# Expert rows of a routed layer: gathered in quarters of the tokens and transposed by VectorE instead of TensorE

## The reference, cut to what matters

```python
scores = jnp.maximum(x @ gate_W + gate_b, 1e-4)
p = softmax(scores)                       # 8 experts, the best 2 are kept
w = maximum(p, 0.1) / (sum of the two kept)
y = einsum('bsd,edf->bsef', x, expert_W) + expert_b
out = einsum('bsef,bse->bsf', y, comb) / 2
x = x + out
```

## Time and profile before

| | before |
|---|---|
| median of three runs | 1190.6 us |
| the profiled execution | 1190.14 us, span 1188.3 us |
| mean granted TensorE clock | 0.984 |
| PE / DVE / ACT / POOL busy | 1148.8 / 587.7 / 308.7 / 462.5 us |
| part from the first expert matmul to the end | from 896.5 us of the span |

### The profile page before, as it was taken

How to read it: one execution, slowest core, us unless ns; L and a number is a source line. 1 busy time by engine, 2 the same in 40 slices (tenths; PEclk the granted TensorE clock), 3 DMA queues, 4 the chain that set the end, 5 groups by cost and what they waited for, 6 DMA issues and landing times.

```text
span 1188.3 us, 15152 instructions
## 1 busy us (share of the span) xinstructions
PE 1148.8 (97%) x5588; PEld 984.9 (83%) x5588; DVE 587.7 (49%) x1171; ACT 308.7 (26%) x416; POOL 462.5 (39%) x394
## 2 busy tenths in 40 slices
PE   6999999999999999999999999999959999999996
PEld 5898888888788999999988878888847788788884
DVE  7935666555332122211133447997589622744444
ACT  2421212133111121211022213343353411623232
POOL 0003457457787577511000015233323444443433
PEclk9999999999999999999999999999968999999998
DMA  9382785783634444477457633463288954876653
GB/s 355 114 347 50 204 226 117 232 210 36 137 48 43 93 93 94 97 159 153 92 175 244 204 109 116 166 243 131 94 297 307 336 87 91 257 235 128 190 88 72
DMA packets 115835, 192.15 MB, mean 162 GB/s; under 512 B 33960, under 2 KB 63912, under 8 KB 114624
## 3 DMA queue, kind: packets, MB, share of 16 engines
q1 hardware_dynamic: 81008, 159.53, 39.0%
q0 software_dynamic: 34768, 31.82, 19.8%
HBM read 136.19 MB, written 61.68 MB: 167 GB/s over the span
## 4 chain that ended last, share of the span: by engine, by line
PE 89%; DVE 8%; issue 1%; ACT 1%; DMA 0%; DVEq 0%; POOL 0%; ACTq 0%; POOLq 0%
PE ps L1564 28%; PE ps L1565 28%; PE ps L1566 28%; DVE e_lo L1389 2%; PE ps L1783 2%; PE ps L1712 2%; PE ps L1652 2%; DVE xn_lo L1116 1%; DVE stats L1088 1%; DVE acc L1104 1%; PE ps L1610 1%; DVE y L1534 0%; ACT lt_hi L1012 0%; DMA acc<-in_x 0%; DVE tok_w L1503 0%
## 5 line engine op out<-in xcount | busy, mean ns | idle before, releaser
L734 POOL DMA_INDIRECT cnt_d<-times,addr_i x160 | 263.0, 1644 | 179.1 <-DMA cnt_d<-times,addr_i 96.0
L1564 PE MATMUL ps<-e_hi,lt_hi 128*128 128x512 f32 x368 | 148.0, 402 | 2.8 <-DVE e_lo L1389 2.3
L1566 PE MATMUL ps<-e_hi,lt_lo 128*128 128x512 f32 x368 | 144.1, 392 | 0.0
L1565 PE MATMUL ps<-e_lo,lt_hi 128*128 128x512 f32 x368 | 144.1, 391 | 0.0
L1565 PE MATMUL ps<-xt_lo,q_hi 128*128 128x416 f32 (+1 forms) x384 | 135.0, 352 | 0.0
L1564 PE MATMUL ps<-xt_hi,q_hi 128*128 128x416 f32 (+1 forms) x384 | 135.0, 351 | 0.0
L1566 PE MATMUL ps<-xt_hi,q_lo 128*128 128x416 f32 (+1 forms) x384 | 134.6, 351 | 0.0
L842 POOL DMA_INDIRECT out<-y,row_put x46 | 73.7, 1602 | 87.8 <-ACT y L1046 51.4
L1564 PEld LDWEIGHTS ps<-e_hi,lt_hi 128*128 128x128 f32 x368 | 69.6, 189 | 23.2 <-DVE e_lo L1389 9.0
L1257 DVE TENSOR_TENSOR qs<-ps,qs 128x416 f32<-128x416 f32 (+1 forms) x24 | 14.2, 592 | 136.9 <-PE ps L1566 136.9
L1566 PEld LDWEIGHTS ps<-e_hi,lt_lo 128*128 128x128 f32 x368 | 69.5, 189 | 14.9
(11 more groups left out here) (257 smaller groups left out, 2382.0 us busy)
## 6 DMA issues: line engine op xcount, KB each, us to landing
e_raw<-in_L_ffn_expert_W SPq DMA_DIRECT2D x64, 512.0 KB, 9.8
cnt_d<-zeros SPq DMA_DIRECT2D x20, 640.0 KB, 12.2
rows<-key_d SPq DMA_DIRECT2D x8, 1250.0 KB, 7.5
acc<-in_x SPq DMA_DIRECT2D x18, 512.0 KB, 7.5
w_raw<-in_L_mix_w_key SPq DMA_DIRECT2D x16, 512.0 KB, 4.4
cnt_d<-cnt_d POOLq DMA_DIRECT2D x10, 640.0 KB, 7.6
cnt<-cnt_d SPq DMA_DIRECT2D x10, 640.0 KB, 5.9
h_d<-hs SPq DMA_DIRECT2D x18, 256.0 KB, 2.3
```

Source lines behind the costliest of these rows:

```text
L734: nc.gpsimd.indirect_dma_start(out=cnt_d[i], out_offset=bass.IndirectOffsetOnAxis(ap=addr_i[:, j:j + 1], axis=0), in_=times[:, j:j + 1], i ...
L1564: nc.tensor.matmul(o, lh, rh, start=(k == 0), stop=False)
L1565: nc.tensor.matmul(o, lh, rl, start=False, stop=False)
L1566: return nc.tensor.matmul(o, ll, rh, start=False, stop=(k == last_k))
```

## The change

The rows stored in HBM have their 1024 columns in another order, so that each row falls into four pieces of 256 columns: piece q holds columns 32q to 32q+31 of every group of 128. The gate's weights are loaded in a matching order, by eight DMAs instead of one. In the loop, POOL gathers a block in four indirect DMAs of 128 pieces of 1 KB. The t-th of them is for tokens 32t to 32t+31, and brings to partitions 32q to 32q+31 the q-th pieces of these tokens. The 32x32 transposes of VectorE, 256 columns at a time and straight into PSUM banks 4 and 5, then give the whole transposed block. The indices for this (`quad_of`) come from four small matmuls with shifted unit matrices (`sel`). TensorE's transposes leave the loop. Only the first block is still gathered whole; ACT puts its columns back in order (`gp`) in two copies, and TensorE transposes it.

The small copies of indices (`tok_now`, `row_put`) go from POOL to DVE. In DVE's loop, the four transposes, each with its copy of the next indices, stand at the start of an iteration, ahead of the bias of the left half. POOL's loop holds six indirect DMAs and waits only. In SP's stream one weight piece of the third expert waits for the first block's transposes, because `gp` is stored in its place.

The diff, cut to its core:

```diff
+    QD = 32
+    NQD = P // QD
+    QK = D // NQD
+        sel = at("sel", X + HALF, [P, NQD, P], f16)
+        gp = at("gp", RING + (2 * KB - 1) * D, [P, KB, P])
 # SP
                     if running is not None and k == AT_ONCE:
-                        sp.wait_ge(s_gx, first_block[running] * 16 + 32)
+                        sp.wait_ge(s_gx[NQD - 1], first_block[running] * 16 + 16)
...
-                    sp.dma_start(gw[:, :, :], gate_W.rearrange("(k p) e -> p k e", p=P)).then_inc(s_gw, 16)
+                    for c in range(NQD):
+                        for g in range(2):
+                            sp.dma_start(gw[c * QD:(c + 1) * QD, g:KB:2, :],
+                                         gate_W[(g * NQD + c) * P:(g * NQD + c + 1) * P, :].rearrange("(q i) e -> i q e", q=NQD)).then_inc(s_gw, 16)
...
-            sp.wait_ge(s_gx, 16)
-            load_expert(2, range(KB))
+            sp.wait_ge(s_gx[0], 16)
+            load_expert(2, range(KB - 1))
+            sp.wait_ge(s_tr, 2)
+            load_expert(2, range(KB - 1, KB))
 # POOL
+            def gather_quarter(t, index):
+                nc.gpsimd.indirect_dma_start(out=gx[:, t * QK:(t + 1) * QK], out_offset=None,
+                                             in_=xn2_d.rearrange("n (b k) -> (n b) k", b=NQD),
+                                             in_offset=bass.IndirectOffsetOnAxis(ap=index, axis=0)).then_inc(s_gx[t], 16)
...
-            pool.wait_ge(s_tr, 2)
-            gather_rows(tok_of[:, 1:2])
+            pool.wait_ge(s_gp, 2)
+            pool.wait_ge(s_tok, 1)
+            for t in range(NQD):
+                gather_quarter(t, quad_of[:, t, 1:2])
...
             with pool.Fori(0, blocks) as i:
-                pool.wait_ge(s_tr, i * 2 + 4)
-                nc.gpsimd.tensor_copy(tok_now[:, :], tok_of[:, bass.ds(i + 2, 1)]).then_inc(s_tok, 1)
-                pool.wait_ge(s_tok, i + 1)
-                pool.sem_inc(s_passed, 1)
-                gather_rows(tok_now[:, :])
+                for t in range(NQD):
+                    pool.wait_ge(s_tok, i * NQD + (t + 2))
+                    pool.sem_inc(s_passed, 1)
+                    gather_quarter(t, tok_now[:, t, :])
                 for h in range(NH):
                     c = slice(h * HALF, (h + 1) * HALF)
-                    pool.wait_ge(s_sc[h], i * 16 + 16)
-                    pool.sem_inc(s_passed, 1)
-                    nc.gpsimd.tensor_copy(row_put[:, h:h + 1], row_of[:, h, bass.ds(i, 1)]).then_inc(s_put, 1)
-                    pool.wait_ge(s_put, i * 2 + (1 + h))
+                    pool.wait_ge(s_put, i * NH + (h + 1))
                     pool.sem_inc(s_passed, 1)
                     pool.wait_ge(s_y[h], i + 2)
 # ACT
+            act.wait_ge(s_gx[0], 16)
             for g in range(2):
-                block_hi(0, g)
+                nc.scalar.copy(gp[:, MB * g:MB * g + MB, :].rearrange("p c (q i) -> p c q i", q=NQD),
+                               gx[:, :].rearrange("p (q c i) -> p c q i", q=NQD, c=KB)[:, MB * g:MB * g + MB, :, :]).then_inc(s_gp, 1)
+            for g in range(2):
+                act.wait_ge(s_tr, g + 1)
+                block_hi(g)
...
+                        if h == 0:
+                            act.wait_ge(s_turn, (i + 1) * NQD)
                         act.wait_ge(s_mm, i * 3 + (2 + h))
-                        block_hi(i + 1, h)
+                        block_hi(h)
 # DVE, ahead of the loop
-                    nc.vector.tensor_scalar(xn2[0:w, i % 2, :], x2v, mv[0:w, 0:1], nt1[0:w, :],
+                    nc.vector.tensor_scalar(xn2[0:w, i % 2, :].rearrange("p (q c i) -> p c q i", q=NQD, c=KB),
+                                            x2v.rearrange("p (c q i) -> p c q i", q=NQD, c=KB), mv[0:w, 0:1], nt1[0:w, :],
                                             ALU.subtract, ALU.mult).then_inc(s_xn2, 1)
+                if t == NT - 1:
+                    for q in range(NQD):
+                        V.tensor_copy(sel[:, :, q * QD:(q + 1) * QD], ident[:, :].rearrange("p (t j) -> p t j", t=NQD))
...
+            for q in range(NQD):
+                V.memset(quad[q * QD:(q + 1) * QD, :], float(q))
...
+            V.tensor_scalar(tok_f[:, :], ps[:, 2, 0:NSLOT], -1.0, 0.0, ALU.add, ALU.max).then_inc(s_route, 1)
...
+            def quarter_turned(t):
+                V.transpose(ps[:, 4:6, :].rearrange("p g (c t j) -> p (g c) t j", c=MB, t=NQD)[:, :, t, :],
+                            gx[:, t * QK:(t + 1) * QK].rearrange("p (c i) -> p c i", c=KB)).then_inc(s_turn, 1)
...
+            dve.wait_ge(s_tokp, 2)
+            V.tensor_scalar(quad_of[:, :, :], ps[:, 3, 0:NQD * NSLOT].rearrange("p (t s) -> p t s", t=NQD), float(NQD), quad[:, 0:1],
+                            ALU.mult, ALU.add).then_inc(s_tok, 1)
 # DVE, loop (right_weighed first)
                     dve.wait_ge(s_sc[1], i * 16 + 16)
+                    dve.sem_inc(s_passed, 1)
+                    V.tensor_copy(row_put[:, 1:2], row_of[:, 1, bass.ds(i, 1)]).then_inc(s_put, 1)
...
                 with dve.Fori(first_block[e], first_block[e + 1]) as i:
+                    dve.wait_ge(s_llo, i * 2 + 2)
+                    dve.sem_inc(s_passed, 1)
+                    for t in range(NQD):
+                        dve.wait_ge(s_gx[t], i * 16 + (32 if t == 0 else 16))
+                        dve.sem_inc(s_passed, 1)
+                        quarter_turned(t)
+                        V.tensor_copy(tok_now[:, t, :], quad_of[:, t, bass.ds(i + 2, 1)]).then_inc(s_tok, 1)
                     for h in range(NH):
...
+                        if h == 0:
+                            dve.wait_ge(s_sc[0], i * 16 + 16)
+                            V.tensor_copy(row_put[:, 0:1], row_of[:, 0, bass.ds(i, 1)]).then_inc(s_put, 1)
 # PE
+            pe.wait_ge(s_route, 2)
+            for t in range(NQD):
+                last = nc.tensor.matmul(ps[:, 3, t * NSLOT:(t + 1) * NSLOT], sel[:, t, :], tok_f[:, :], start=True, stop=True)
+            last.then_inc(s_tokp, 1)
...
-                    last = nc.tensor.transpose(ps[:, 4 + g, b * P:(b + 1) * P], gx[:, k * P:(k + 1) * P], ident[:, :])
+                    last = nc.tensor.transpose(ps[:, 4 + g, b * P:(b + 1) * P], gp[:, k, :], ident[:, :])
...
-                        if h == 0:
-                            pe.wait_ge(s_gx, i * 16 + 32)
-                            pe.wait_ge(s_llo, i * 2 + 2)
-                            for b in range(2):
-                                block_transposes(b)
```

More of the change, by code:

```diff
@@ L45, in gps_layer @@
     AT_ONCE = 3
+    QD = 32
+    NQD = P // QD
+    QK = D // NQD
+    assert KB * QD == QK
     F32_MAX = 3.4028234e38
@@ L237, in gps_layer @@
         slot_f = gate("slot_f", [P, NSLOT])
-        slot_e = gate("slot_e", [P, NSLOT])
+        quad_of = gate("quad_of", [P, NQD, NSLOT], i32)
+        sel = at("sel", X + HALF, [P, NQD, P], f16)
+        gp = at("gp", RING + (2 * KB - 1) * D, [P, KB, P])
         row_of = at("row_of", RAW + 2 * NT * NE, [P, NH, NSLOT], i32)
@@ L275, in gps_layer @@
         last_c = at("last_c", EX + 3 * D, [P, NE, NSLOT], f16)
-        tok_now = small("tok_now", [P, 1], i32)
+        tok_now = small("tok_now", [P, NQD, 1], i32)
+        tok_f = small("tok_f", [P, NSLOT], f16)
+        quad = small("quad", [P, 1])
         row_put = small("row_put", [P, NH], i32)
@@ L439, in gps_layer @@
         s_ehi, s_elo = sem("s_ehi"), sem("s_elo")
-        s_gx, s_tok, s_tr, s_lhi, s_llo, s_mm, s_ye = (sem(n) for n in (
-            "s_gx", "s_tok", "s_tr", "s_lhi", "s_llo", "s_mm", "s_ye"))
+        s_gp, s_tok, s_tr, s_lhi, s_llo, s_mm, s_ye = (sem(n) for n in (
+            "s_gp", "s_tok", "s_tr", "s_lhi", "s_llo", "s_mm", "s_ye"))
         s_passed = sem("s_passed")
+        s_gx = [sem(f"s_gx{t}") for t in range(NQD)]
+        s_turn = sem("s_turn")
         s_put, s_y, s_sc = sem("s_put"), [sem(f"s_y{h}") for h in range(2)], [sem(f"s_sc{h}") for h in range(2)]
@@ L808, in gather_rows @@
                 nc.gpsimd.indirect_dma_start(out=gx[:, :], out_offset=None, in_=xn2_d,
-                                             in_offset=bass.IndirectOffsetOnAxis(ap=index, axis=0)).then_inc(s_gx, 16)
+                                             in_offset=bass.IndirectOffsetOnAxis(ap=index, axis=0)).then_inc(s_gx[0], 16)
+            def gather_quarter(t, index):
+                nc.gpsimd.indirect_dma_start(out=gx[:, t * QK:(t + 1) * QK], out_offset=None,
+                                             in_=xn2_d.rearrange("n (b k) -> (n b) k", b=NQD),
+                                             in_offset=bass.IndirectOffsetOnAxis(ap=index, axis=0)).then_inc(s_gx[t], 16)
             gather_rows(tok_of[:, 0:1])
@@ L844, in _ @@
                                                  in_=y[:, c], in_offset=None, compute_op=ALU.add).then_inc(s_sc[h], 16)
-            pool.wait_ge(s_gx, blocks * 16 + 32)
-            pool.sem_inc(s_passed, 1)
+            for t in range(NQD):
```

(11 more changed lines are left out.)

## The result

The changed kernel takes **1188.05 us** (median of 7 runs, 1186.12 to 1190.13); the kernel before, on the same chips, 1191.08 (7 runs, 1190.09 to 1192.53). The ratio is 0.9975, 95% interval 0.9963 to 0.9987: 3.0 us faster. The prediction had 1186.2, which is 4.4 us under the 1190.6 that it started from. Run again later: 1188.09 (7 runs), ratio 0.9974 [0.9963, 0.9985]. One execution of experiment 11 took 1441.7 us at a mean granted clock of 0.744, where its other five took 1214.4 to 1217.4 at 0.972 to 0.976, and is left out of its ratio.

A forecast was written before the change was run, and what follows sets the result against it. TensorE was taken as the bound (89% of the chain), DVE as equally late at experts' starts. Terms -13.8 - 0.9 - 0.5 + 9.5 + 1.3 = -4.4 us gave 1185.7 on the profiled execution, 1186.2 as median; range 1182 to 1201.

The forecast's parts named there:

- Transposes off TensorE: TensorE's loop: each plain block goes from 11.80 to 10.88 us, 0.92 less; 15 plain blocks give -13.8 us.
- Turns on DVE: DVE's loop: four transposes with copies take 1.8 us per block, free in plain blocks; blocks 10, 16, 21 +1.75 each.
- The first rival: DVE's turns cost 2.5 to 3.4 us per block, mainly at experts' starts: 1190 to 1196, around 1192; chance 0.20.
- A block behind a start: Blocks 3, 12 and 17 were counted as plain blocks, -0.92 us each, with nothing for the preceding start's pause.
- Blocks 1 and 2: First two expert starts in the loop: DVE's added work makes block 1 +1.5 us and block 2 +1.35.
- the two `row_put` copies add 0.2: DVE's loop: the two index copies moved from POOL cost 0.2 us per block, besides the transposes' 1.8.
- the rival at 0.04: TensorE's clock falls in new pauses at six places, 1.8 us for nine matmuls, 11 us in all: 1197; chance 0.04.
- Two of the prediction's own signs of being wrong: Prediction wrong if transposes exceed 0.5 us each, DVE waits for the `gx` DMA in plain blocks, or the clock falls.
- the rival of gathers landing late (0.08): Experts' starts: gathers land in 9.3 us, not 4.4, `lt_lo` 1 to 2 late after six blocks: 1192 to 1198; chance 0.08.
- predicted -5.2: The loop, blocks 1 to 22 together: predicted change in the time between `yb` right starts, in us.
- Before the first block: Ahead of the loop: DVE's added copies and memsets cost +1.3 us, bounds 0.5 and 3; first matmul about 897.8.
- GpSimd: POOL's loop: 0.30 us per start, 9.1 per block; rival, chance 0.13: above 0.61 POOL sets pace, 12.3 us turns, about 1205.

The follow-up runs named there:

- experiment 11: Changed kernel with the left half's scatter ahead of the four gathers in GpSimd's loop: 1216.79 us, ratio 1.0213 to the kernel before.
- experiment 6: Changed kernel with every quarter turned twice on DVE, first into two unused PSUM banks: 1194.97 us, ratio 1.003 to the kernel before.
- experiment 7: Changed kernel with each turn doing only 32 of its 256 columns: 1186.36 us, ratio 0.9956 to the kernel before.
- experiment 4: Changed kernel without gathers, turns, `lt_hi` or `lt_lo` for blocks that don't exist: 1185.58 us, ratio 0.9954 to the kernel before.
- experiment 1: Changed kernel with DVE's left-half `row_put` copy and its wait moved behind `lt_lo`: 1188.22 us, ratio 0.9971 to the kernel before.
- experiment 2: Changed kernel with five of the next expert's pieces moved behind the first block's turns and `yb`: 1183.5 us, ratio 0.9933 to the kernel before.
- experiment 3: Changed kernel with the edits of experiment 1 and experiment 2 together: 1183.64 us, ratio 0.9934 to the kernel before.
- experiment 8: Changed kernel with the edits of experiment 2 and experiment 4 together: 1182.75 us, ratio 0.9922 to the kernel before.
- experiment 10: Kernel before the change, with only the new order of the `e_lo` pieces from experiment 2: 1204.47 us, ratio 1.0109 to the unedited kernel before.
- Experiment 5: Changed kernel with the `tok_now` and `row_put` copies back on GpSimd, each before its transfer: 1251.8 us, ratio 1.0493 to the kernel before.
- experiment 9: Changed kernel run again unedited, for the second profile: 1188.09 us, ratio 0.9974 to the kernel before.

## Why the prediction was nearly right, step by step

- **Transposes off TensorE: right.** Twelve plain blocks go from 11.80 to 10.88, the predicted 0.92. The loop's pure matmul time is now the pace.
- **Turns on DVE: right, a little cheap.** 1.55 us for the four instead of 1.8; blocks 10, 16 and 21 became 1.14 longer, not 1.75, and block 11 1.10, not 1.35. Together 2.1 us better than predicted. Experiments 6 and 7 show that this time is paid at the starts and not in plain blocks. The estimate of 2.5 us, worked out from the figure in the Trainium skill ("VectorE: DVE Perf Modes", the section on the three transpose paths), was not borne out: 1.55 us. The doubling price (0.33 us for 256 columns) and the cut price (0.236 less for 224 columns, 1.05 ns a column) match the slope that the prediction took from other operations. The first rival, dearer turns at 0.20, is out.
- **A block behind a start: missed.** Blocks 3 and 12 take 11.35 to 11.39, 0.5 more than plain, as the pause of a start reaches into them; block 17 does too (11.35 with the clock held, experiment 4). 1.0 us for the two, which the sum had at nothing.
- **Blocks 1 and 2: the term that was mis-sized.** Predicted +2.85 together; +5.9 in the first profile, +4.5 in the second. The prediction counted only DVE's work there. GpSimd was behind as well, four gathers ahead of the scatter, whose landing held the index copy; and in the first profile the clock was down behind the 4.67 us pause besides. Pieces that came late inside block 2 (1.32 us in the second profile) were not in the sum at all. The wait that the change put on DVE ("the two `row_put` copies add 0.2") is longer than the copy whenever the scatter is late: 2.45 to 3.48 us in three of five profiles. It was costed as a copy and not as a wait. On the time of the whole kernel this wait shows no price of its own, though: experiment 1 moved it and gained nothing.
- **The clock: the rival at 0.04 came true in part.** In the loop of the first profile it is down in blocks 2 and 17, of the second in blocks 11, 17 and 22. It costs 1.6 us at block 17 (12.92 and 12.97, against 11.35 in experiment 4), 0.75 at block 22 and nothing at block 11. The price for one place, 1.8 us, was near; treating it as all six places or none was not.
- **Two of the prediction's own signs of being wrong appeared.** The clock fell, as just said. And in three plain blocks (3, 12 and 17) DVE's turns did wait for the DMA into `gx`, for 4.0, 4.9 and 2.1 us in all in the first profile. That is the rival of gathers landing late (0.08), which in the changed kernel came without its price, since DVE had the time; with shorter turns such waits, and one for the scatter, reached TensorE in block 12 (experiment 7). So the number came out within the range with part of the mechanism missed.
- **The loop's account (first profile).** -0.8 against the predicted -5.2, 4.4 short: block 1 +2.2 over its prediction, block 17 +2.0 (1.6 clock, 0.5 the pause ahead of it), blocks 3 and 12 +1.0, block 2 +0.8, block 22 +0.3, and the cheaper turns -2.1; that sums to 4.2, the rest is rounding.
- **Before the first block: dearer than need be in the sum, and hidden by the clock.** The first matmul stood at 898.97, predicted 897.8. Block 0's `yb` right comes at 910.05 to 910.10 in the profiles of experiments 1, 2 and 4, 0.4 before that of the kernel before, and at 911.0 to 912.1 in both profiles of the changed kernel and in experiments 3 and 8. In these the clock stood at 0.50 for all of 868 to 870 (0.80 to 0.92 in the three, 0.88 before), ahead of the gate's last matmuls, and DVE's chain on the scores began 1 to 2 us later. This delay isn't the change's: experiment 10 has the early fall, and the scores at 877.20, with the kernel before's program. From the scores (877.30) to `lt_lo` (898.02) it took 20.72 us, 20.42 before: 0.3 of own work, not 1.2. The copies of `sel`, put at 0.8, stand ahead of that chain, at 841.9, and take 0.5. Block 0 itself went from 13.94 us (first matmul to `yb` right) to 12.89, 1.05 less, where the prediction had 0.5.
- **GpSimd: right.** 0.30 us ahead of nearly every gather, with the decision at 0.61. Ahead of a scatter it is 0.30 only where `y` was ready long before; where it waits for `y`, it starts 0.83 to 0.85 us behind it, which costs nothing as long as GpSimd has slack. Experiment 5 is the rival made real (+63.8 us; blocks 5 to 9 of 13.5 to 14.1, more than the rival's 12.3, as a gather there takes 2.08 us from start to start, its copy of 0.2 included, and not 1.86).
- **The end: not in the sum, and luck.** From the last `yb` right to the end of the span it is 0.7 us less than before in the first profile and 1.3 less in the second. That is in spite of GpSimd's gathers for blocks that don't exist, which stand ahead of the last scatters and which experiment 4 prices at 2.5 us: the last scatter starts 3.8 us behind that `yb`, before 3.0. Why the end is shorter all the same stays open.

All together, first profile: block 0 ends 1.4 us later, the loop is 0.8 shorter and the end 0.7, so the span is the same, where -4.4 was predicted. On medians it is 1188.05 measured and 1186.2 predicted. So part of the nearness is luck: cheaper turns (2.1 us) and the shorter end (0.7) stand against blocks 1 and 2 (3.0), block 17 (2.0) and blocks 3 and 12 (1.0), and the profiled execution of the changed kernel is 2.1 us above its median, that of the kernel before 0.9 below its own. The split above is known for the profiled executions alone; the second profile has most of the same places, and block 22 and block 2 with other sizes.

## What to carry to other kernels

Work taken off the bounding engine pays where the engine that gets it has slack, and costs where it has none: here 12 blocks gained 0.92 us each and the starts of experts gave back most of it, and reordering DVE's queue at these starts (experiment 2) was worth more (5.0 us) than the transfer itself (3.0). Cost a moved wait as a wait, with what is queued behind it on an in-order engine, and not as the small instruction that it guards. An order that helps one kernel can hurt the next: the same one was worth 5 us in the changed kernel and cost 13 in the one before, where the pieces came to stand behind a wait of 3.6 us.

## What the runs showed of the hardware

- A transpose on VectorE of 128x256 fp32 in blocks of 32 from SBUF to PSUM takes 0.446 us (median of 92), 0.388 us from start to start with a one-column copy between (changed kernel); one of 128x32 takes 0.22 us, 0.152 with the copy (experiment 7).
- A gather of 1 KB pieces had landed 3.0 us after its issue (median; 2.6 to 7.0), one of whole rows in the kernel before 4.4: with a quarter of the bytes the median is a third shorter.
- GpSimd started an indirect DMA 0.30 us behind the one before it when its wait was long met, 0.79 to 0.86 us behind its own small copy in most cases (experiment 5), and 0.83 to 0.85 us behind the end of the `y` that it waited for.
- The scatter of a half block landed 4.6 to 5.6 us after its start in most blocks, and 8.1 to 9.1 us after it in blocks 0, 1, 9 and 15 (changed kernel, first profile).
- TensorE's granted clock fell to 0.50 behind pauses of 2.25 us and held behind equal ones, at the same place in two executions of the same kernel (block 11, experiment 9).
